# The causal mask product opens the score banks of an attention step, and the row-tiled score products add to it

## The reference, cut to what matters

```python
scores = jnp.einsum('bhqd,bhkd->bhqk', qh, kh) / math.sqrt(hd)   # 16 heads of 16 features
causal = ki <= qi
scores = jnp.where(causal[None, None], scores, jnp.asarray(MASKED_BIAS, scores.dtype))
attn = jax.nn.softmax(scores, axis=-1)
out = jnp.einsum('bhqk,bhkd->bhqd', attn, vh)
```

## Time and profile before

| | |
|---|---|
| runs before, us | 901.8 (median), 900.1, 901.93 |
| profiled execution, us | 902.15, of which the span from first to last instruction is 900.4 |
| TensorE matmul busy | 804.4 us, 89% of the span |
| VectorE busy | 615.5 us, 68% |
| ScalarE busy | 320.0 us, 36% |
| GpSimd busy | 168.0 us, 19% |
| mean granted TensorE clock | 0.957 of full speed |
| stage C | from 480.6 to about 617 us of the span |

### The profile page before, as it was taken

How to read it: one execution, slowest core, us unless ns; L and a number is a source line. 1 busy time by engine, 2 the same in 40 slices (tenths; PEclk the granted TensorE clock), 3 DMA queues, 4 the chain that set the end, 5 groups by cost and what they waited for, 6 DMA issues and landing times.

```text
span 900.4 us, 14122 instructions
## 1 busy us (share of the span) xinstructions
PE 804.4 (89%) x4803; PEld 650.9 (72%) x4803; DVE 615.5 (68%) x1196; ACT 320.0 (36%) x515; POOL 168.0 (19%) x173
## 2 busy tenths in 40 slices
PE   2877878599999999999998899987699999999994
PEld 2565657488888888888885566655588788888883
DVE  5999999664564466466546888886446675867754
ACT  2120212123433342342233777756053323324221
POOL 1899999500000000000000010100010010100000
PEclk9999999999999999999998999976589999999997
DMA  7221212000000000001001112110000000000000
GB/s 269 71 88 47 71 45 65 19 1 1 1 0 0 0 0 0 0 0 36 14 1 44 51 54 85 53 36 2 0 1 1 1 23 0 0 23 0 24 1 24
DMA packets 20436, 25.92 MB, mean 29 GB/s; under 512 B 3632, under 2 KB 15920, under 8 KB 20272
## 3 DMA queue, kind: packets, MB, share of 16 engines
q1 hardware_dynamic: 20400, 25.47, 8.9%
HBM read 23.36 MB, written 2.10 MB: 28 GB/s over the span
## 4 chain that ended last, share of the span: by engine, by line
PE 67%; DVE 19%; issue 7%; ACT 3%; POOL 1%; DVEq 1%; DMA 1%; SPq 0%; ACTq 0%; POOLq 0%
PE bank L1566 24%; PE bank L1428 20%; PE bank L1441 10%; DVE A L856 2%; DVE small L1050 2%; PE bank L1495 2%; DVE A L845 2%; PE bank L1481 2%; PE bank L1575 2%; ACT A L618 1%; DVE A L1060 1%; PE bank L1506 1%; PE bank L1485 1%; PE bank L1535 1%; PE bank L1353 1%
## 5 line engine op out<-in xcount | busy, mean ns | idle before, releaser
L1566 PE MATMUL bank<-R 128*128 128x512 f32 (+4 forms) x1104 | 220.0, 360 | 9.7 <-DVE R L1212 4.9
L1566 PEld LDWEIGHTS bank<-R 128*128 128x128 f32 (+2 forms) x1104 | 180.7, 185 | 48.5 <-DVE R L1212 5.2
L1428 PE MATMUL bank<-R 128*128 128x512 f32 (+1 forms) x816 | 198.0, 392 | 1.9 <-issue 1.9
L1428 PEld LDWEIGHTS bank<-R 128*128 128x128 f32 (+1 forms) x816 | 146.7, 185 | 33.2 <-issue 2.2
L997 DVE TENSOR_TENSOR A<-bank,A 128x512 f32<-128x512 f32 (+1 forms) x68 | 47.0, 691 | 118.7 <-PE bank L1428 118.6
L1441 PEld LDWEIGHTS bank<-R 128*128 128x128 f32 (+1 forms) x816 | 105.8, 190 | 10.7 <-issue 4.0
L1441 PE MATMUL bank<-R 128*128 128x256 f32 (+1 forms) x816 | 109.4, 283 | 2.5 <-DVE R L1008 2.1
L560 ACT ACTIVATE A<-bank 128x512 f32<-128x512 f32 (+1 forms) x68 | 40.7, 599 | 194.7 <-PE bank L1428 194.7
L1353 PE MATMUL bank<-A 128*128 128x256 f32 x128 | 43.5, 422 | 29.4 <-DVE A L845 19.3
L432 POOL TENSOR_TENSOR A<-A 128x256 f32<-128x256 f32 x64 | 63.7, 995 | 10.4 <-DVE A L856 10.4
L1176 DVE TENSOR_TENSOR A<-bank,A 128x512 f32<-128x512 f32 (+1 forms) x48 | 32.9, 686 | 35.3 <-PE bank L1566 35.0
(11 more groups left out here) (170 smaller groups left out, 1141.7 us busy)
## 6 DMA issues: line engine op xcount, KB each, us to landing
A<-in_w SPq DMA_DIRECT2D x17, 384.0 KB, 3.1
A<-in_w SPq DMA_DIRECT2D x8, 480.0 KB, 3.6
A<-in_ctx_one SPq DMA_DIRECT2D x8, 272.0 KB, 3.6
A<-in_ctx_half SPq DMA_DIRECT2D x8, 256.0 KB, 3.2
A<-in_ctx_nat SPq DMA_DIRECT2D x4, 512.0 KB, 3.6
A<-in_ctx_t SPq DMA_DIRECT2D x128, 16.0 KB, 2.0
out<-X SPq DMA_DIRECT2D x4, 512.0 KB, 2.9
A<-in_filt SPq DMA_DIRECT2D x1, 1536.0 KB, 11.5
```

What stands on the lines that cost most here:

```text
L1428: mm = nc.tensor.matmul(dst[0:pr], wX[:, j, at + k * P:at + k * P + pr], mX[:, k], start=(n == 0), stop=(n == 5))
L1566: mm = nc.tensor.matmul(dst, a, m, start=start and n == 0, stop=stop and n == len(prods) - 1, skip_group_check=skip)
```

## The change

The mask pair moves ahead of the loop over the score products. The mask products now open the accumulation of each bank (start), all score products add to it, and the last score product carries the signal `scores_ready`. The waits at the head of `c_scores` stay where they are.

```diff
                 u = k % 2
+                for c in range(2):
+                    nc.tensor.matmul(S_[u][:, c * 512:(c + 1) * 512], identb[:], neg[:], start=True, stop=False,
+                                     skip_group_check=True)
                 for kk in range(DT):
                     for c in range(2):
                         rows = slice((2 * u + c) * QR, (2 * u + c + 1) * QR)
-                        nc.tensor.matmul(S_[u][:, c * 512 + kk * 2 * P:c * 512 + (kk + 1) * 2 * P],
-                                         qT[rows, b, kk], kbd[rows, r, b % 2, kk],
-                                         start=(kk == 0), stop=False, skip_group_check=True)
-                for c in range(2):
-                    mm = nc.tensor.matmul(S_[u][:, c * 512:(c + 1) * 512], identb[:], neg[:], start=False, stop=True,
-                                          skip_group_check=True)
+                        mm = nc.tensor.matmul(S_[u][:, c * 512 + kk * 2 * P:c * 512 + (kk + 1) * 2 * P],
+                                              qT[rows, b, kk], kbd[rows, r, b % 2, kk],
+                                              start=False, stop=(kk == 1), skip_group_check=True)
                 mm.then_inc(scores_ready, 1)
```

## The result

The changed kernel took 914.26 us (median of four runs, 914.06 to 915.06) against 901.14 (900.10 to 901.93) before: a ratio of 1.0148, with an interval of 1.0133 to 1.0162. The forecast was 902.3, and its range ended at 904.7.

A forecast was written before the change was run, and what follows sets the result against it. The prediction took the attention's chain to go round TensorE, VectorE and ScalarE, with expert-layer matmuls the largest shares overall. Terms 0.42 + 0.19 - 0.14 = +0.47 us on 901.8 gave 902.3 us, range 900.4 to 904.7.

The forecast's parts named there:

- points 1 to 5: Attention score passes: price of a shape change, time to scores ready, to next product, cover by waits, stage ends; sum +0.47 us.
- The change part by part: Its first paragraph, on the score step: counts and waits stay, nothing starts earlier, only TensorE's queue is touched; no size given.
- point 4: Transposes behind the scores: waits for exponentials cover the 0.14 us a step, except three times on the chain, 0.42 us.
- The sign that the prediction set for itself: Group of eight attention steps: forecast wrong if it moves by more than 0.4 us either way; about 30.3 us expected.
- A: Transposes behind the scores: waits fail to cover, 0.14 us in each of 32 steps, 4.5 us, 906.3 us; chance 0.10.
- B: Mask after value products: weights load early, tiles to full array costs nothing, 0.09 off at 12 passes, 901.2 us; chance 0.18.
- C: Lower clock stretch ends at another step, 2.4 us each: one more 904.7, chance 0.09; one fewer 899.9, chance 0.08.

The follow-up runs named there:

- run 1: Changed kernel, GpSimd's second split of each group held back about 0.3 us by four semaphore increments: 898.85 us, ratio 0.9986 to the kernel before.
- run 3: Kernel before, old order, with one more mask product of 512 columns per step ahead of the mask pair: 912.00 us, ratio 1.0119.
- run 4: Changed kernel without the clamp of the row maximum: 895.84 us, ratio 0.9940 to the kernel before.
- run 5: Changed kernel with each GpSimd split of 960 columns written as four of 240: 898.43 us, ratio 0.9986 to the kernel before.

## Why the prediction was wrong

*The order's price* (points 1 to 5) was right but for a few hundredths. The distances came out within 0.01 us, and 0.14 a group was forecast where 0.18 and 0.21 were measured. At the stage's start VectorE's maximum came 4.85 us behind the transposes in place of 4.93 (-0.08, forecast -0.14); in the last group it came 11.08 behind them in place of 10.90 (+0.18, forecast +0.19).

*The step that failed* is the first paragraph of "The change part by part", that no queue other than TensorE's is touched, and with it point 4, which took the 0.14 us that reach the chain as a price and nothing more. I followed that delay along TensorE and into the exponentials, but not into VectorE's place beside GpSimd. GpSimd's split is started by ScalarE, behind an exponential of the step before; the clamp hangs on the scores that follow the late transposes. So the delay moved one and not the other. Counted from the first transposes of a group, the split starts at 8.42 us (518.20 - 509.78) where it started at 8.40 (547.98 - 539.58), and the clamp at 8.43 where it started at 8.26: from 0.14 us ahead to 0.01 behind. The sign that the prediction set for itself, a group moved by more than 0.4 us, came up with 3.79. A forecast that listed what runs beside each late VectorE instruction would have seen a margin of the very size of the delay.

The trace of before held the warning. In its last group the clamp already stood behind the split:

```profile
593.38 1.95 DVE L1054 TENSOR_SCALAR small<-small 128x8 f32<-128x8 f32 x1
...
593.08 2.22 POOL L461 TENSOR_TENSOR R<-A,R 128x960 f32 x1 [12.66 <-ACT R L613]
```

The chain that the prediction read goes through this clamp (1.87 us at 593.46), and I passed over its length. The changed kernel has this stall as well, 1.93 us at 605.09, so it is no part of the difference.

*The account of a group:* 33.98 - 30.19 = 3.79 us are 0.18 for the order (run 1), 2.23 - 0.17 = 2.06 for the stall, and a rest of 1.55, which is close to the 1.40 that the lower clock cost in run 3. The step behind the stall bears it out: from 522.94 to 528.18 it takes 5.24 us, and the same step of run 3's first group, at a clock of 1.00, takes 527.20 - 523.26 = 3.94 with a mask product of 0.23 more in it.

*The rivals.* A (every step pays) fell: eight steps at 0.14 would be 1.12 us a group, and the order by itself cost 0.18 to 0.21; the waits of the transposes stay, 0.42 to 0.44 us at the heads of the groups. B (no price for the change from tiles to full array) fell: the mask came 0.58 behind the values. C had the right symptom: the lower clock comes three times more inside stage C. But it had the wrong size and left the stall out; the clock falls behind the stall, and in runs 1, 4 and 5, which have the same order and no stall or a short one, it is 1.00 over the first two whole groups.

## What to carry to other kernels

A delay of a tenth of a microsecond is priced by what it moves past, and not only by its length: for each instruction made late, look for a long instruction on another engine that starts just behind it. Here a VectorE operation of 0.17 us that reads and writes SBUF (the on-chip memory of the tiles) was worth 3.6 us a group, the slower clock behind it counted in, because a GpSimd instruction of 2.2 us got in first. Three ways out were measured: dropping the small operation where the result allows it, cutting the GpSimd work beside it into pieces, or holding that work back. A blocked instruction shows as busy and not as waiting, so look for it in durations: 0.17 us in one step and 2.23 in another for the same line.

## What the runs showed of the hardware

These VectorE instructions waited for a GpSimd subtraction of two SBUF operands: the clamp, 2.23 us in place of 0.17, and the addition with two operands in SBUF, 0.96 in place of 0.42. The subtraction that reads PSUM took its 1.23 us beside it. The Trainium skill, SBUF — State Buffer, section "Who interferes with whom", says that VectorE's second port pair is shared with GpSimd, that `tensor_scalar` can enter a mode that contends for it, that two SBUF inputs contend with a GpSimd instruction that reads SBUF, and that whoever issues first gets it for the whole instruction. The traces agree for VectorE's side: 0.14 or 0.03 us ahead the clamp paid nothing, 0.01 to 0.30 behind it waited for the rest of that one instruction, 2.2 us of 960 columns or 0.7 of 240. They don't show the port or the mode, and not the other side either: 0.03 us behind the clamp GpSimd's split took its usual 2.23 us.
